# A token-mixing layer with attention over heads and eight experts: token groups re-cut, P transposed by DVE, V copied by ACT

## What is computed

```
xn = layernorm(x)
xp = silu(xn @ W_in.T)
alpha, beta, v = sigmoid(xp @ W_alpha.T + b), sigmoid(xp @ W_beta.T + b), tanh(xp @ W_v.T + b)
h_t = alpha_t * h_(t-1) + beta_t * v_t          # scan over the 4096 tokens
x = x + (h * silu(h)) @ W_out.T
u = layernorm(x);  g = rmsnorm(u)
q = g @ Wq + bq                                 # 16 heads of 64
k, v = split((g @ Wdown + bdown) @ Wup + bup)   # 16 heads of 64 each
att = softmax(q[t,h] . k[t,g] / 8 over g)       # per token: 16 x 16, heads against heads
u = u + (att @ v) @ Wo + bo
h2 = rmsnorm(u);  gate = softmax(h2 @ Wg + bg)  # 8 experts
x = x + u + sum_e gate_e * (h2 @ We_e)
```

## Time and profile before

| | |
|---|---|
| median of 3 runs | 2071.92 us (2069.83 to 2075.27) |
| the profiled execution's own time | 2072.49 us |
| its span, slowest core (core 2) | 2069.7 us (the others from 2058.9) |
| PE busy, core 2 | 1954.5 us, 94% |
| DVE busy | 1229.8 us, 59% |
| ACT busy | 721.7 us, 35% |
| POOL busy | 223.2 us, 11% |
| mean granted clock, by core | 0.973 to 0.975 |

### The profile page before, as it was taken

How to read it: one execution, slowest core, us unless ns; L and a number is a source line. 1 busy time by engine, 2 the same in 40 slices (tenths; PEclk the granted TensorE clock), 3 DMA queues, 4 the chain that set the end, 5 groups by cost and what they waited for, 6 DMA issues and landing times.

```text
span 2069.7 us, 33009 instructions; the slowest of 8 cores (2058.9 to 2069.7 us)
## 1 busy us (share of the span) xinstructions
PE 1954.5 (94%) x11520; PEld 914.0 (44%) x11520; DVE 1229.8 (59%) x2055; ACT 721.7 (35%) x1905; POOL 223.2 (11%) x225
## 2 busy tenths in 40 slices
PE   4666699999999999999999999999999999999899
PEld 2223344444444444445444444444444444444444
DVE  5447446864577546775468645775467754675544
ACT  2226432533443333542325334433335423342100
POOL 5443100110002100020001100020000200011000
PEclk9876699999999999999999999999999999999999
DMA  8999875665533354334543354333543344433344
GB/s 249 311 315 176 159 196 175 174 173 179 188 113 132 123 204 153 132 123 147 199 143 123 123 185 181 121 125 123 205 162 122 123 153 153 143 102 123 118 147 163
DMA packets 49317, 334.25 MB, mean 161 GB/s; under 512 B 5939, under 2 KB 6067, under 8 KB 14326
## 3 DMA queue, kind: packets, MB, share of 16 engines
q1 hardware_dynamic: 41974, 270.92, 37.6%
q0 software_dynamic: 7184, 61.23, 12.3%
HBM read 317.86 MB, written 48.23 MB: 177 GB/s over the span
## 4 chain that ended last, share of the span: by engine, by line
PE 89%; DMA 5%; DVE 2%; issue 2%; POOL 1%; ACT 1%; DVEq 0%; SPq 0%; ACTq 0%; POOLq 0%
PE bank L359 41%; PE bank L414 14%; PE bank L460 6%; PE bank L542 5%; PE bank L428 5%; PE bank L399 5%; DMA we<-wall 2%; PE bank L489 2%; PE bank L515 2%; PE bank L525 2%; PE bank L476 2%; DMA wscr<-wm 1%; PE bank L512 1%; PE bank L441 1%; PE bank L449 1%
## 5 line engine op out<-in xcount | busy, mean ns | idle before, releaser
L359 PE MATMUL bank<-we,h2T 128*128 128x512 bf16 x4096 | 938.1, 379 | 9.9 <-DVE gat L909 6.5
L712 DVE SCALAR_TENSOR_TENSOR xs<-bank,gat,xs 128x512 f32<-128x512 f32 x512 | 383.9, 750 | 442.3 <-PE bank L359 442.0
L359 PEld LDWEIGHTS bank<-we,h2T 128*128 128x128 bf16 x4096 | 386.8, 98 | 435.8 <-issue 21.0
L414 PE MATMUL bank<-F,wm 128*128 128x512 bf16 x1536 | 339.4, 383 | 20.9 <-POOL wm L278 20.1
L291 POOL TENSOR_TENSOR pb<-pb,sml 128x512 bf16<-128x512 bf16 x128 | 132.9, 1039 | 1440.9 <-DVE sml L841 1440.9
L667 ACT ACTIVATE pb<-bank,sml 128x128 bf16<-128x128 f32 x512 | 181.2, 367 | 217.3 <-DVE sml L833 207.0
L414 PEld LDWEIGHTS bank<-F,wm 128*128 128x128 bf16 x1536 | 151.4, 99 | 207.8 <-issue 31.4
L428 PE MATMUL bank<-wm,F 128*128 128x512 bf16 x512 | 113.7, 384 | 12.0 <-POOL wm L278 12.0
L542 PE MATMUL bank<-wm,F 128*128 128x512 bf16 x512 | 123.2, 384 | 0.7 <-DVE F L870 0.7
L781 DVE SCALAR_TENSOR_TENSOR R<-R 128x512 f32<-128x512 f32 x64 | 49.5, 774 | 122.6 <-ACT R L622 122.6
L460 PE MATMUL bank<-F,wm 128*128 128x512 bf16 x512 | 121.6, 380 | 0.0
(11 more groups left out here) (93 smaller groups left out, 1645.8 us busy)
## 6 DMA issues: line engine op xcount, KB each, us to landing
we<-wscr SPq DMA_DIRECT2D x128, 1024.0 KB, 4.8
wm<-wscr SPq DMA_DIRECT2D x98, 1024.0 KB, 5.9
wscr<-wall POOLq DMA_DIRECT2D x16, 1024.0 KB, 13.0
out<-xs SPq DMA_DIRECT2D x32, 512.0 KB, 4.3
wscr<-wm POOLq DMA_DIRECT2D x14, 1024.0 KB, 25.5
xs<-x SPq DMA_DIRECT2D x7, 2048.0 KB, 10.8
xs<-wall POOLq DMA_DIRECT2D x12, 1024.0 KB, 23.3
we<-wall POOLq DMA_DIRECT2D x10, 1024.0 KB, 23.1
```

The source lines that it names most:

```text
L359: mm = pe.matmul(b[:, :], hT[:, kc * 512 + tb * 128:kc * 512 + (tb + 1) * 128], we[ui % NE][:, kc * 512:(kc + 1) * 512], start=(kc == 0), ...
L414: mm = pe.matmul(bk[(mc % 2) * 3 + j][:, :], w[:, (ci % 4) * 1024 + kc * 128:(ci % 4) * 1024 + (kc + 1) * 128], F2[:, kc * 512:(kc + 1) * ...
L712: v.scalar_tensor_tensor(dst, bk[6 + k % 2][:, :], gat[(t - 1) % 2][:, tb * 8 + e:tb * 8 + e + 1], dst, OP.mult, OP.add).then_inc(v_ec, 1)
```

## The change

A group now holds the tokens i * 64 + g, i = 0 to 7, that is tokens 64 apart, and `qt`, `kt` and `vt` are stored as (part i, head, group g). One head's evacuation is then eight runs of 64 columns; the 128 columns of one group stand 64 elements (128 bytes) apart, and PE takes them so in the scores and in V's transposes, as weights or as columns. The order inside a group is part, then head, so the 16 columns of one token stand side by side and P is block diagonal in blocks of 16. DVE transposes P in 32x32 blocks from `pb` into `pt` (in place of PE's transposes and of the copy of P). V's transposes move ahead on PE, behind the scores of the same j; ACT copies them out of PSUM into `vb`, three buffers. The cast into F1 writes runs of 4 and reads its bank in steps of 64. `qm` and `km` are built for the new layout on the host, with the same sizes. DVE's order within a step is rearranged.

Lines below with a number are those of the changed program, one to five more than before for the same statement: L490 is the scores, L504 V's transposes, L527 P·V, L360 the expert block, L858 the DVE transpose, L837 and L845 the reduce and reciprocal, L717 the expert addition, L728 the statistics, L873 the cast; ACT's copy of V is L667 there and the exponential L672.

The diff:

```diff
     pb = [sb(f"pb{i}", [128, 512], BF16) for i in range(3)]
-    ptv = [sb(f"ptv{i}", [128, 768], BF16) for i in range(2)]
+    pt = [sb(f"pt{i}", [128, 512], BF16) for i in range(2)]
+    vb = [sb(f"vb{i}", [128, 256], BF16) for i in range(3)]
...
@@ -487,46 +488,47 @@
                 for g in range(4):
                     gg = j * 4 + g
                     mm = pe.matmul(bk[j % 2][:, g * 128:(g + 1) * 128],
-                                   qt[0:72, gg * 128:(gg + 1) * 128],
-                                   kt[0:72, gg * 128:(gg + 1) * 128], start=True, stop=True)
+                                   qt[0:72, :].rearrange("p (n g) -> p g n", g=64)[:, gg],
+                                   kt[0:72, :].rearrange("p (n g) -> p g n", g=64)[:, gg],
+                                   start=True, stop=True)
                 mm.then_inc(p_s, 1)
 
-            ec(t, A_S0)
-            score(0)
-            ec(t, 1)
-            score(1)
-            ec(t, 1)
-            for j in range(16):
-                if j + 2 < 16:
-                    score(j + 2)
-                ec(t, 1)
+            def vtr(j):
                 if j == 0:
                     pe.wait_ge(a_vv, t * 8 + 8)
                     pe.wait_ge(v_vd, t * 8 + 8)
                 if j >= 2:
-                    pe.wait_ge(v_ptv, t * 16 + j - 1)
-                pe.wait_ge(g_pn, t * 16 + j + 1)
-                bb = bkb[2 + j % 2]
+                    pe.wait_ge(a_vb, t * 16 + j - 1)
                 for g in range(4):
                     gg = j * 4 + g
-                    pe.transpose(bb[:, 512 + g * 64:512 + (g + 1) * 64],
-                                 vt[0:64, gg * 128:(gg + 1) * 128], idb[0:64, 0:64])
-                for g in range(4):
-                    mm = pe.transpose(bb[:, g * 128:(g + 1) * 128],
-                                      pb[j % 3][:, g * 128:(g + 1) * 128], idb[:, :])
-                mm.then_inc(p_ptv, 1)
+                    mm = pe.transpose(bkb[2 + j % 2][:, g * 64:(g + 1) * 64],
+                                      vt[0:64, :].rearrange("p (n g) -> p g n", g=64)[:, gg],
+                                      idb[0:64, 0:64])
+                mm.then_inc(p_vt, 1)
+
+            ec(t, A_S0)
+            for j in range(2):
+                score(j)
+                vtr(j)
                 ec(t, 1)
-                pe.wait_ge(v_ptv, t * 16 + j + 1)
+            for j in range(16):
+                if j + 2 < 16:
+                    score(j + 2)
+                    vtr(j + 2)
+                ec(t, 1)
+                pe.wait_ge(v_pt, t * 16 + j + 1)
+                pe.wait_ge(a_vb, t * 16 + j + 1)
                 if j >= 2:
                     pe.wait_ge(v_o, t * 16 + j - 1)
                 bo = bk[4 + j % 2]
+                pv = pt[j % 2][:, :].rearrange("p (g i l u) -> p g l i u", i=8, l=2, u=8)
                 for g in range(4):
                     for hl in range(2):
                         mm = pe.matmul(bo[64 * hl:64 * hl + 64, g * 64:(g + 1) * 64],
-                                       ptv[j % 2][:, 512 + g * 64:512 + (g + 1) * 64],
-                                       ptv[j % 2][:, g * 128 + hl * 64:g * 128 + (hl + 1) * 64],
+                                       vb[j % 3][:, g * 64:(g + 1) * 64], pv[:, g, hl],
                                        start=True, stop=True)
                 mm.then_inc(p_o, 1)
+                ec(t, 1)
             ec(t, A_WO)
             w0 = wait_m(m0 + 12)
             w1 = wait_m(m0 + 13)
@@ -645,24 +647,27 @@
                          bias=cph[:, 48:49]).then_inc(a_z, 1)
             for mc in range(NCH):
                 s.wait_ge(p_wq, t * 8 + mc + 1)
-                qv = qt[0:64, :].rearrange("p (g s) -> p g s", s=128)
+                qv = qt[0:64, :].rearrange("p (i h g) -> p h i g", i=8, h=16)
                 for hl in range(2):
                     h = 2 * mc + hl
-                    off = hl * 64 + mc * 8
-                    r = s.activation(out=qv[:, :, off:off + 8],
-                                     in_=bk[mc % 2][64 * hl:64 * hl + 64, :].rearrange("p (g i) -> p g i", i=8),
+                    r = s.activation(out=qv[:, hl * 8 + mc],
+                                     in_=bk[mc % 2][64 * hl:64 * hl + 64, :].rearrange("p (i g) -> p i g", i=8),
                                      func=AF.Identity, scale=0.125, bias=cph[:, h:h + 1])
                 r.then_inc(a_q, 1)
                 hd = 2 * mc
                 s.wait_ge(p_wup, t * 16 + hd + 1)
-                vv = vt[0:64, :].rearrange("p (g s) -> p g s", s=128)
-                s.activation(out=vv[:, :, hd * 8:hd * 8 + 8],
-                             in_=bk[(3, 4, 5, 2)[hd % 4]][64:128, :].rearrange("p (g i) -> p g i", i=8),
+                vv = vt[0:64, :].rearrange("p (i h g) -> p h i g", i=8, h=16)
+                s.activation(out=vv[:, mc],
+                             in_=bk[(3, 4, 5, 2)[hd % 4]][64:128, :].rearrange("p (i g) -> p i g", i=8),
                              func=AF.Identity, bias=cph[:, 32 + hd:33 + hd]).then_inc(a_vv, 1)
             for j in range(16):
+                s.wait_ge(p_vt, t * 16 + j + 1)
+                if j >= 3:
+                    s.wait_ge(p_o, t * 16 + j - 2)
+                s.activation(out=vb[j % 3][:, :], in_=bkb[2 + j % 2][:, 0:256], func=AF.Copy).then_inc(a_vb, 1)
                 s.wait_ge(v_mx, t * 16 + j + 1)
                 if j >= 3:
-                    s.wait_ge(p_ptv, t * 16 + j - 2)
+                    s.wait_ge(v_pt, t * 16 + j - 2)
                 for g in range(4):
                     r = s.activation(out=pb[j % 3][:, g * 128:(g + 1) * 128],
                                      in_=bk[j % 2][:, g * 128:(g + 1) * 128], func=AF.Exp,
@@ -818,14 +823,13 @@
             for hd in range(16):
                 v.wait_ge(p_wup, t * 16 + hd + 1)
                 b = bk[(3, 4, 5, 2)[hd % 4]]
-                kv = kt[0:64, :].rearrange("p (g s) -> p g s", s=128)
-                v.tensor_scalar_add(kv[:, :, hd * 8:hd * 8 + 8],
-                                    b[0:64, :].rearrange("p (g i) -> p g i", i=8),
+                off = (hd % 2) * 8 + hd // 2
+                kv = kt[0:64, :].rearrange("p (i h g) -> p h i g", i=8, h=16)
+                v.tensor_scalar_add(kv[:, off], b[0:64, :].rearrange("p (i g) -> p i g", i=8),
                                     cph[:, 16 + hd:17 + hd]).then_inc(v_k, 1)
                 if hd % 2 == 1:
-                    vv = vt[0:64, :].rearrange("p (g s) -> p g s", s=128)
-                    v.tensor_scalar_add(vv[:, :, hd * 8:hd * 8 + 8],
-                                        b[64:128, :].rearrange("p (g i) -> p g i", i=8),
+                    vv = vt[0:64, :].rearrange("p (i h g) -> p h i g", i=8, h=16)
+                    v.tensor_scalar_add(vv[:, off], b[64:128, :].rearrange("p (i g) -> p i g", i=8),
                                         cph[:, 32 + hd:33 + hd]).then_inc(v_vd, 1)
 
             def smax(j):
@@ -848,15 +852,15 @@
             ec(t, 1)
             rsum(0)
             for j in range(16):
+                v.wait_ge(g_pn, t * 16 + j + 1)
+                if j >= 2:
+                    v.wait_ge(p_o, t * 16 + j - 1)
+                v.transpose(pt[j % 2][:, :], pb[j % 3][:, :]).then_inc(v_pt, 1)
                 if j + 2 < 16:
                     smax(j + 2)
-                ec(t, 1)
                 if j + 1 < 16:
                     rsum(j + 1)
-                v.wait_ge(p_ptv, t * 16 + j + 1)
-                if j >= 2:
-                    v.wait_ge(p_o, t * 16 + j - 1)
-                v.tensor_copy(ptv[j % 2][:, :], bkb[2 + j % 2][:, 0:768]).then_inc(v_ptv, 1)
+                ec(t, 1)
                 if t + 1 < NT:
                     if j < 8:
                         ln1_bn(t + 1, j)
@@ -864,11 +868,11 @@
                         ln1_aggr(t + 1)
                     if j == 10:
                         ln1_nm(t + 1)
+                v.wait_ge(p_o, t * 16 + j + 1)
+                ov = F1[:, :].rearrange("p (u i g) -> p u i g", u=8, i=8)[:, :, :, j * 4:(j + 1) * 4]
+                v.tensor_copy(ov, bk[4 + j % 2][:, 0:256].rearrange("p (g i u) -> p u i g", u=8, i=8)
+                              ).then_inc(v_o, 1)
                 ec(t, 1)
-                v.wait_ge(p_o, t * 16 + j + 1)
-                ov = F1[:, :].rearrange("p (u g i) -> p g u i", u=8, i=8)[:, j * 4:(j + 1) * 4]
-                v.tensor_copy(ov, bk[4 + j % 2][:, 0:256].rearrange("p (g u i) -> p g u i", u=8, i=8)
-                              ).then_inc(v_o, 1)
             ec(t, A_WO)
             for u in range(8):
                 sl = slice(u * 512, (u + 1) * 512)
@@ -966,11 +970,7 @@
     cph[:, 16:32] = bup[:, 0, :].T
     cph[:, 32:48] = bup[:, 1, :].T
     cph[:, 48] = arr("L0_ffn_bdown")
-    qm = np.zeros((8, 128), np.float32)
-    km = np.zeros((8, 128), np.float32)
-    for r in range(8):
-        qm[r, r::8] = 1.0
-        km[r, r::8] = MASKV
```

(5 more changed lines are left out.)

6 lines of the change are left out of this document (3 added, 3 removed).

## The result

| | before | with the change |
|---|---|---|
| median of 4 runs each | 2072.66 us | 2168.95 us |
| ratio, 95% interval | | 1.0452 [1.0432, 1.0471] |
| span of the profiled execution | 2069.7 us | 2164.7 us (core 7; its own time 2166.36) |
| PE busy | 94% | 95% |

The change makes the kernel 4.5% slower, by 96 us. I had forecast 44 (2116, range 2038 to 2160): the sign was right, the size outside the range.

The account below looks back on a forecast made before the run. The prediction took PE's own sequence, busy 94%, to bound the kernel. Stepped reads +72, P's transposes −27 and tile 0 −1 gave +44 us on 2072.49: 2116 us, range 2038 to 2160.

Parts of the forecast that it names:

- Part 1: P's transposes leave PE: four matmuls, 0.24 us per attention step in tiles 1 to 7, 27 us less.
- Part 2: DVE transposes P at 0.68 us in place of the 0.44 us copy, hidden behind PE's expert blocks: no cost.
- my two bounds: The cast on DVE: from no change (0.41 us long) to 0.35 us more.
- Part 3: ACT copies V, 256 elements per step, under 0.68 us each, covered by ACT's idle half: no cost.
- Part 4: Evacuations of q, k, v write runs of 64 instead of eight: no gain, q's stays at 0.68 us.
- Part 5: PE's stepped reads in scores and V's transposes, at 1.34 ns a column: 0.64 us per step, 72 us more.
- Rival 3: Separate weight columns cost like streamed ones or more: 2238 at GpSimd's pace, 2159 at DVE's; chance 0.11 for over 2140.
- Rivals 1 and 2: PE's stepped reads at full pace, 2044 us, chance 0.32; at half pace, 2076 us, chance 0.16.
- Part 6: Tile 0's attention, without expert blocks: waits set the step, 14 steps × 0.07, 1 us less.
- The ring: Tile 0's loop of waits: transpose, reduce, reciprocal, GpSimd's scaling of the next P; 2.81 us a step before, 2.74 forecast.

## Why the prediction was right in sign and wrong in size

**What bounds the kernel.** Right. PE's own sequence sets seven of eight tiles; six of them went from 82.28 to between 95.1 and 95.6 us, 16 × 0.80 = 12.8 of it by the longer step, and no wait of over 0.5 us took part in it.

**Part 1, P's transposes off PE: −27.** Right, less a piece. With reads side by side the step is 4.36 instead of 4.58 us, 0.22 × 112 = 25 us. That kernel gave 20 and not 28, since the first P·V of each tile waits 0.9 for the transpose. I had checked P·V's wait for a step in full swing (where it holds: in the kernel with reads side by side, no wait after the first) and not for the first one, whose reciprocal stands on DVE behind the expert addition of the block before. The change hides it under its slow scores.

**Part 2, DVE's transpose at 0.68.** Right: 703 ns. The cast did not slow (410 ns), the lower of my two bounds. DVE is idle twice a step, 1.28 and 1.00 us, and PE does not wait for it in tiles 1 to 7 of the change.

**Part 3, ACT's copy: nothing.** Right: 384 ns, and its 5.3 us of waits at P·V all lie in tile 0.

**Part 4, longer runs: nothing.** Right, 684 and 684, and now with its reason: runs of 2 are as fast as runs of 64, runs of 1 cost 2434.

**Part 5, stepped reads: +72. This is the step that failed.** I took "DVE's BN_STATS: 684 ns for 512 elements", 1.34 ns each, as PE's pace, and carried the ratio 3.05 over to weights. Measured are 1.7 ns for a streamed column alone in its 16 bytes, and q's weights, which I had taken for hidden behind the scores, add 0.11 to it. Scores rise by 0.76 to 0.77 (I had 0.46), V's transposes by 0.26 (0.18), together 1.03 against 0.64 a step, 115 us against 72. The neighbour that I chose was the fault: BN_STATS takes its 512 elements side by side, so its figure says nothing on how fast PE can take lone columns from memory. The time for lone columns also hardly knows PE's clock. In tile 0, at a granted clock of 0.50, PE's timeline has

```profile
196.26 1.21 PE L490 MATMUL bank<-kt,qt 72*128 72x128 bf16 x4
197.40 0.57 PE L504 MATMUL bank<-idbs,R 64*128 64x64 bf16 x4
```

that is 1.14 us for the scores, against 1.08 at full clock, where before they took 0.54 and 0.23. So the price over packed columns is smaller at the lower clock (0.60 instead of 0.85 by these rows). Rival 3 had the right mechanism for weights in part (a price of their own) and a price too high: 2159 at DVE's pace for both. The Trainium skill (TensorE: Matmul & The Clock Gate, Weight-path perf modes) lets the fast weight load take columns in steps of up to 1,024 elements; read as no price for such steps, as I did, it would have given 2096. For V's transposes the traces disagree: 0.22 up to step 2, 0.37 at 8 to 32, 0.48 at 64. Rivals 1 and 2 fall with a read at 218 ns for 128 columns instead of 56 or 107.

**Part 6, tile 0: −1.** Right: 50.99 to 49.64 us. The ring by POOL's starts is 196.34 to 199.07, 2.73 where I had worked out 2.74. Slower scores lay beside it as I said.

**What I left out: tile 1.** I wrote that SP and POOL have "the same transfers in the same order, waiting for the same counts", and stopped there. Order and counts are the same, the moments are not: PE's slower steps shifted when a load was issued, to just behind a conversion. 8.75 us on the slowest core.

**Sum.** 115 (reads) − 25 (P's transposes) − 1 (tile 0) + 9 (tile 1) = 98, measured 96. The range ended at 2160 with 2168.95 measured; reads alone at their right price would have given 2072.5 + 115 − 28 = 2159.5, the very edge of it. So of the miss of 53 us the price of the reads is 43, and tile 1's loss, for which I had no term, about 9.
